# Interleaving the next head group's q/k/v projections with attention, splitting a chain of small loads, and moving the global gate behind the first matmul block in a fused two-layer kernel

## The reference

```python
# layer 0, attention branch: 32 heads of 32 channels, full attention
q, k, v = split(xn @ w_qkv)
attn = softmax(q @ k.T * 32**-0.5)
s = layernorm((attn @ v) @ w_out + b_out) * gamma + beta
# layer 0, feed-forward branch: two sub-layers, each local attention and then
h = shift_token(x); h = layernorm(h) * lg + lb
a, g = split(h @ w1 + b1)                 # hidden size 2730
x = x + (a * gelu(g)) @ w2 + b2
# layer 1, feed-forward branch: a global gate and three coupling cycles
gf = sigmoid(gelu(gelu(mean(x) @ g1 + gb1) @ g2 + gb2) @ g3 + gb3)
for _ in range(3):
    tf = sigmoid(net4(out))               # 1024-1024-512-256-1, gelu between
    coupling = 0.1 + ar * (0.7 * gf + 0.3 * tf - 0.5) * 2
    out = out + coupling * twist(out)
```

## Time and profile before

| | us |
|---|---|
| median of 2 runs (lowest, highest) | 10630.68 (10603.10, 10658.27) |
| the profiled execution's own time | 10745.24 |
| its span on the slowest core (core 4) | 10743.7 |
| spans of the eight cores in it | 10634.7 to 10743.7 |
| TensorE busy / VectorE busy / ScalarE busy | 5844.8 / 3108.8 / 2104.9 |
| mean granted TensorE clock, share of full | 0.648 |

### The profile page before, as it was taken

The page is one execution under the profiler, slowest core; times in us unless marked ns, Lnnn a source line. Parts: engine busy times, 40 slices in busy tenths (PEclk is TensorE's granted clock), DMA queues, the critical chain, the costliest instruction groups (busy, mean ns, idle before and its releaser), DMA issues.

```text
span 10743.7 us, 58525 instructions; the slowest of 8 cores (10634.7 to 10743.7 us)
## 1 busy us (share of the span) xinstructions
PE 5844.8 (54%) x17052; PEld 1814.1 (17%) x17240; DVE 3108.8 (29%) x4213; ACT 2104.9 (20%) x2326; POOL 410.3 (4%) x506
## 2 busy tenths in 40 slices
PE   2577877778753455326664554506666215735540
PEld 0122122221211111002221111102222001211110
DVE  3222222222233555211101555402111231112222
ACT  0244544435420122000000211100000110002210
POOL 0000000000000000001111000001111000000000
PEclk9766666666655555567776655557777557767765
DMA  2200000000002000214455000034444241020003
GB/s 77 35 3 0 3 3 3 3 0 0 0 20 64 3 0 0 79 19 43 44 51 99 4 2 0 4 88 42 42 42 42 80 140 43 24 62 0 0 18 139
DMA packets 508711, 356.28 MB, mean 33 GB/s; under 512 B 445968, under 2 KB 450715, under 8 KB 498162
## 3 DMA queue, kind: packets, MB, share of 16 engines
q0 software_dynamic: 441280, 160.70, 13.2%
q1 hardware_dynamic: 67122, 191.82, 5.0%
HBM read 378.92 MB, written 104.86 MB: 45 GB/s over the span
## 4 chain that ended last, share of the span: by engine, by line
PE 43%; DMA 18%; DVE 17%; ACT 13%; issue 7%; DVEq 1%; ACTq 0%; SPq 0%; POOLq 0%
ACT p_at L370 8%; PE p_ps_o L389 7%; PE p_ps_out L942 4%; DMA p_w1g<-f_w 3%; DMA p_w1a<-f_w 3%; PE p_ps_a L908 3%; PE p_ps_m L1335 2%; PE p_ps_b L379 2%; DVE p_ssum L623 2%; DVE p_rec L708 2%; PE p_ps_g L915 2%; PE p_ps_s L363 2%; PE p_ps_o L699 2%; ACT p_at L688 2%; PE p_ps_av L1155 1%
## 5 line engine op out<-in xcount | busy, mean ns | idle before, releaser
L370 ACT ACTIVATE p_at<-p_ps_s,p_m8v 128x1024 bf16<-128x1024 f32 x1024 | 1141.1, 1114 | 1463.7 <-PE p_ps_s L363 1374.6
L363 PE MATMUL p_ps_s<-p_qT,p_kT 32*128 32x512 bf16 x2048 | 854.9, 520 | 325.5 <-ACT p_at L370 314.3
L389 PE MATMUL p_ps_o<-p_at,p_vsb 128*33 128x512 bf16 x2048 | 796.6, 572 | 0.0
L908 PE MATMUL p_ps_a<-p_xh,p_w1a 128*128 128x512 bf16 (+1 forms) x1378 | 487.3, 514 | 534.0 <-DMA p_w1g<-f_w 454.0
L398 DVE RECIPROCAL p_rec<-p_ps_o 1x512 f32<-1x512 f32 x128 | 428.7, 3349 | 613.2 <-PE p_ps_o L389 613.2
L677 PE MATMUL p_ps_s<-p_qTb,p_kTb 64*128 64x512 bf16 x448 | 244.9, 574 | 525.2 <-ACT p_at L688 416.8
L931 DVE SCALAR_TENSOR_TENSOR p_acts<-p_ps_a,p_b1av,p_gbuf 128x512 bf16<-128x512 f32 (+1 forms) x176 | 132.1, 750 | 1158.0 <-ACT p_gbuf L928 1156.7
L688 ACT ACTIVATE p_at<-p_scr,p_m30v 128x512 bf16<-128x512 f32 x448 | 323.2, 722 | 598.5 <-DVE p_scr L683 577.4
L942 PE MATMUL p_ps_out<-p_acts,p_w2sb 128*128 128x512 bf16 (+1 forms) x1376 | 385.0, 438 | 80.0 <-DVE p_xf L948 61.3
L915 PE MATMUL p_ps_g<-p_xh,p_w1g 128*128 128x512 bf16 (+1 forms) x1382 | 405.1, 443 | 2.9 <-issue 1.3
L928 ACT ACTIVATE p_gbuf<-p_ps_g,p_b1gv 128x512 bf16<-128x512 f32 (+1 forms) x176 | 120.9, 687 | 1349.8 <-PE p_ps_g L915 1349.7
(11 more groups left out here) (257 smaller groups left out, 5970.9 us busy)
## 6 DMA issues: line engine op xcount, KB each, us to landing
p_w1a<-f_w POOLq DMA_DIRECT2D x168, 256.0 KB, 4.9
p_w1g<-f_w POOLq DMA_DIRECT2D x168, 256.0 KB, 4.1
p_xt<-x SPq DMA_DIRECT2D x32, 512.0 KB
s_xfa<-p_xf SPq DMA_DIRECT2D x16, 1024.0 KB, 3.9
p_xf<-s_xfa SPq DMA_DIRECT2D x16, 1024.0 KB
p_st<-s_s SPq DMA_DIRECT2D x32, 512.0 KB
p_w2sb<-f_w POOLq DMA_DIRECT2D x2, 5376.0 KB, 50.3
s_xnT_f<-p_ch SPq DMA_DIRECT2D x8, 1024.0 KB, 5.1
```

The lines of the kernel that those rows point to most:

```text
L363: m = ev.op("tensor", lambda e, kt=kt, pb=pb, half=half, hbase=hbase, q0=q0, tp=tp: e.matmul(ps_s[pb][:, half * 512:(half + 1) * 512], kT[ ...
L370: e1 = ev.op("scalar", lambda e, pr=pr, pb=pb: e.activation(at[:, pr * 1024:(pr + 1) * 1024], ps_s[pb][:], AF.Exp, bias=m8v[:], scale=floa ...
L389: mavl = ev.op("tensor", lambda e, kt=kt, hh=hh, po=po: e.matmul(ps_o[po][:], vsb[:, kt * 132 + hh * 33: kt * 132 + hh * 33 + 33], at[:, k ...
L908: ma = ev.op("tensor", lambda e, k=k, c=c, t0=t0, buf=buf, sz=sz: e.matmul(ps_a[buf][0:sz, :], w1a[buf][:, k * 128:k * 128 + sz], xh[k][:, ...
```

## The change

There are three parts.

**Attention.** `qT`, `kT` and `vsb` get two buffers, and the memsets become 128. The projections are cut into 24 units by a function `qkv_units`: 8 for q and k, then 16 for v, all in the bank `ps_qk`. A unit's first matmul waits for the casts of the unit before it (`unit_guard`). Group 0 is projected ahead of the loop. In group g the units of group g+1 are taken from a queue at the head of the iterations, two at the head of each of the first eight and one at each of the last eight. The weight loads run one group further ahead.

```diff
+        def qkv_units(g, buf):
+            st = {"qk_done": [], "v_done": []}
+            units = []
+            for (dst, wsb) in ((qT, wq), (kT, wk)):
+                for tc in range(4):
+                    def u(dst=dst, wsb=wsb, tc=tc, buf=buf, st=st):
...
+                                waits=(gw[buf] + lds +
+                                       ([unit_guard[0]] if unit_guard[0] else []))
+                                      if c == 0 else [],
...
+            for t in range(16):
+                def u(t=t, buf=buf, st=st):
+                    mv = None
+                    for c in range(ND):
+                        mv = ev.op("tensor", lambda e, c=c, t=t, buf=buf: e.matmul(
+                            ps_qk[:, 0:128], xn[c][:, t * 128:(t + 1) * 128],
+                            wv[buf][:, c * 128:(c + 1) * 128],
+                            start=(c == 0), stop=(c == ND - 1)),
+                            waits=([unit_guard[0]] if unit_guard[0] else [])
+                                  if c == 0 else [], inc="mm")
...
+                    nfill = 2 if (hh * 4 + qc) < 8 else 1
+                    for _ in range(nfill):
+                        if queue:
+                            queue.pop(0)()
```

**Feed-forward.** `onesb` and `idf` are loaded ahead of `xf`. The sums and squares wait for `ld` up to the last `xf` tile only (`xf_lds`). The write of `xh` waits for all of `ld2`, and the first Gelus for everything. The 44 loads of `b1` alternate between two semaphores:

```diff
             ev.dma("sync", b1av[0:sz, c:c + 1],
-                   b1_i.rearrange("(d o) -> d o", o=1)[c * 128:c * 128 + sz], inc="ld2")
+                   b1_i.rearrange("(d o) -> d o", o=1)[c * 128:c * 128 + sz],
+                   inc="ld2" if c % 2 == 0 else "ld")
             ev.dma("sync", b1gv[0:sz, c:c + 1],
-                   b1_i.rearrange("(d o) -> d o", o=1)[2730 + c * 128:2730 + c * 128 + sz], inc="ld2")
+                   b1_i.rearrange("(d o) -> d o", o=1)[2730 + c * 128:2730 + c * 128 + sz],
+                   inc="ld2" if c % 2 == 1 else "ld")
...
-                    waits=(lds_all + pdone + [mset] + ev.wait_all("vx")) if c == 0 else [],
+                    waits=(xf_lds + pdone + [mset] + ev.wait_all("vx")) if c == 0 else [],
...
                     xh[c][:, t0:t0 + 512], tta[:], lgv[:, c:c + 1], lbv[:, c:c + 1],
-                    ALU.mult, ALU.add), waits=[vb], inc="vx")
+                    ALU.mult, ALU.add), waits=[vb] + ev.wait_all("ld2"), inc="vx")
```

217 lines of the change are left out of this document (115 added, 102 removed).

## The result

| | before | after |
|---|---|---|
| median of the runs (lowest, highest), us | 10648.36 (10588.40, 10700.58), 10 runs | 10428.67 (10360.55, 10492.05), 11 runs |
| ratio, 95% interval | | 0.9787, 0.9751 to 0.9824 |
| TensorE / VectorE busy in the profiled execution, us | 5844.8 / 3108.8 | 5640.5 / 3111.7 |

The ratio is a saving of 227 us (187 to 265). The prediction said 229 and put it on another median: 10402, with a range of 10350 to 10480. Whether the saving is over 2%, which the prediction gave a chance of 0.57, is left open: the ratio says 2.1%, and its interval holds both sides.

The account below looks back on a forecast made before the run. Attention iterations were taken as ScalarE-paced then TensorE-paced stretches, with idle waits in feed-forward on bias loads. Savings of 80 + 137 + 12 = 229 us from 10630.7 gave 10402; range 10350 to 10480, including the first rival.

Parts of the forecast that it names:

- Attention: 80 forecast: Attention: seven group boundaries replaced by work at iteration heads save 93 us, less 13 for memsets and the first v unit.
- The step by which a single v unit costs nothing: Attention heads: a single v unit's 0.61 us is taken back by products at the high clock; priced at 0.
- The step of the cast behind the reciprocal: Attention heads: the first unit's cast queues behind VectorE's 3.35 us reciprocal; the second q/k unit starts 4.46 after the products.
- the q/k pair: Attention heads: two q/k units cost 6.3 us, plus 0.5 for products all at the low clock: 6.8, four per group.
- the fill runs at the low clock: Attention rival: clock falls in the gap between units, second q/k unit takes 3.54, pair costs 8.7; total 10595; chance 0.10.
- Feed-forward: 137 forecast: Two feed-forward stages, each saving 35.4 on bias transfers, 3 on `onesb` and `idf`, 30.3 on block 0's statistics.
- The bias chain: Feed-forward: 44 bias transfers on two semaphores take 2.34 us a pair, 51.5 instead of 86.9, saving 35.4 a stage.
- The normalization behind the landing: Feed-forward: from the last bias landing to block 1's sums only 16.4 us remain of 46.7, saving 30.3 a stage.
- the 3 us for `onesb` and `idf`: Feed-forward: loading them ahead of `xf` frees `lgv` from waiting for the last `xf` tile; worth 0 to 4 us.
- The rival of 3.06 a pair: Feed-forward rival: small transfers side by side take 3.06 us a pair, giving 10433 in total; chance 0.18.
- Coupling net: 12 forecast: Coupling net: casts with hand-over, 11.2 us, move under the loads, and small VectorE operations, about 1, go.
- a warmer gate: Coupling net: the gate run at a higher clock could save some 5 us more.

Follow-up runs that it names:

- the profiles of the parts: Kernel before with only the attention, feed-forward or coupling net part of the change: ratios 0.9873, 0.9892 and 0.9961 to the kernel before.
- the ladder: Kernel before with 0 to 96 extra unread matmuls at the head of attention iterations, by group; one run, 10900.73 us.
- the experiment that turned the two round: Changed kernel with the previous iteration's reciprocal issued behind the first unit's cast at the head, not ahead of it: ratio 0.9644 to the kernel before.
- the kernel with the moved broadcast: Kernel before with the reciprocal's broadcast matmul moved from behind the eighth score pair to behind the fifth: 10545.78 and 10593.78 us in two runs.
- the kernel with one chain: Changed kernel with all 44 bias loads of a feed-forward stage one after the other again: ratio 0.9833 to the kernel before.

## Why the prediction was right

The forecast was 229 us saved, and 227 (187 to 265) were measured. By the profiles of the parts the terms add up to 73 + 130 + 9 = 212, also inside that interval. Each term was a little high. That forecast and ratio lie only 2 us apart is luck, since the interval is 78 us wide.

**Attention: 80 forecast, 73 measured.** The groups after the change take 324.3, 320.9, 320.9 and 324.3 us; 321 was forecast. The step by which a single v unit costs nothing is shown by its rows and by the ladder. The step of the cast behind the reciprocal is shown by the rows and by the experiment that turned the two round. Three sizes inside the q/k pair were off. I took 1.89 for the second unit, from a row at the boundary with the same gap of 2.63 ahead of it; it took 2.7 to 3.1. The first scores behind it ran at the low clock, which puts the products 11.26 us behind them (794.87 less 783.61) instead of 10.83. And I had all 16 products at the low clock, 6.8; they took 5.2 to 5.5. The first two cost about 1.5 and the third brought 1.3 back; that they cancel to 0.2 is luck. I had taken a neighbour's row for a duration and not asked whether its clock would hold too. The traces say when it does: at the boundary of before the products ahead took 6.2 to 6.5 us, so the clock had risen late in them. In the changed loop they take 5.74, 5.50, 5.41 and 5.31 ahead of the four pairs of a group on core 5, and the second units take 2.69, 2.93, 3.02 and 3.12. The boundaries of the kernel with the moved broadcast show the same with the old code.

The rival "the fill runs at the low clock" was thus true in its first half: the clock did fall in the second unit. Its price was wrong, because I had let the products lose their return as well: they took 5.2 to 5.5, not 6.8.

**Feed-forward: 137 forecast, 130 measured.** The bias chain gave 34.8 us (86.9 less 52.1) for 35.4, and the kernel with one chain put it at 30 to 34 a stage. The normalization behind the landing is 16.4, as worked out. The term that failed is the smallest: the 3 us for `onesb` and `idf`. From `onesb` to the first bias load it is 120.2 us (4572.37 less 4452.21), where from the first `xf` to it there were 119.1 before: moving them gained nothing and cost 1 (119.9 and 121.1 as means of all cores and both stages). The rival of 3.06 a pair is gone; that step of the earlier trace rows had weight loads beside it, as was said against it.

The Trainium skill, page "DMA: Bandwidth & Descriptors", section on the two cost components, puts most of a small transfer's 2 us on the receipt. Two in flight at 2.39 a pair agree with it.

**Coupling net: 12 forecast, 8 to 10 measured.** The casts' shadow is there, and more: 15.8 us up to the second layer as a mean of the cores, 12.7 in the rows shown. The prediction named what could cost as much, a table load and a colder block behind the gate, and set it against a warmer gate, at zero together. The gate was at the high clock for the first 16 of its matmuls (1.84) and took 21.5 us (9367.96 less 9346.44), for at most 25.8 before (9663.54 less 9637.74), which is inside the 12.7. The layer behind it lost 5.8 on average, 7.3 in the rows. 1.3 of that is the table load; it is not one more, since each kernel has three on this way, but it has moved from the first block into this layer. The two sides did not come to zero but to a cost of some 2 to 4 us.

**The point on which it hung.** The price of the change in attention was less the work moved than the waits that came with it and what the clock made of both. The forecast put the shift to be "taken back" at half a microsecond by looking at how periods settled in the earlier trace rows; the ladder measures that 1.1 us is still free.

## What to carry to other kernels

Work moved from between stages into a loop is paid at the place in the iteration where it lands: the same projections cost 50 us a group at the heads and nothing inside the score phase, which ScalarE paces up to the fifth pair. When two small pieces of work share a buffer, look at what stands between them on the engine that frees it; one instruction of 3.35 us there cost 3.4 us an iteration. A loop whose products stretch and shrink with the granted clock does not answer one for one, so measure a ladder of added work before trusting a price of a microsecond. A duration taken over from a neighbouring row holds only if what ran ahead of it is the same: with the same gap and the same code, one unit took 1.89 us and another 3.56.

## What the runs showed of the hardware that was not expected

- The period of the attention loop stays at 17.06 us with up to 1.1 us more TensorE work at its head, and settles again only at 20.47 us, with 64 added matmuls. The work is paid by more of the products running at 2.4 instead of 1.2 GHz (6.30 us to 5.31 for 16).
- A gap of 2.63 us does not by itself cost TensorE the high clock. The unit behind it took 1.89 us where the products ahead had run mostly at the low clock (6.2 to 6.5 us for 16), and 3.4 to 3.6 us where the clock had risen early in them (4.8 to 5.0). Behind a gap of 1.01 us, and 1.6 us sooner, a unit behind products of 5.1 to 5.2 us still took 1.89.
- A strided transfer of 2688 single elements and one of 42 behind it took 5.84 us of SP's queue (4530.70 less 4524.86); as 22 transfers in a chain they took about 44.
- The broadcast of 1.9 us, moved to where TensorE waits for ScalarE, let the loop fall into an alternation of 14.51 and 16.16 us, broken by stretches of 16.8 to 17.0.
- What stays open: which of gap and time since the clock rose decides when it falls, since the experiment with the earlier cast changed both; and why the ladder's periods with 32 and 48 matmuls differ between cores by up to 0.6 us.
